# Slot attention and layer norms with centring on TensorE and folded weights; small weights of all stages loaded early

## What is computed

```
c = LN(ctx, lnkv_g, lnkv_b);  k = c @ wk + bk;  v = c @ wv + bv
slots = q_mu + exp(q_logsig) * layernorm(x)
3 times:
  q = LN(slots, lnq_g, lnq_b) @ wq + bq
  attn = softmax over the slots of (q k^T * sqrt(128)) + 1e-8, then divided by its sum over the context
  slots = slots + (attn @ v) @ wu + bu
  slots = slots + gelu(LN(slots, lnm_g, lnm_b) @ w1 + b1) @ w2 + b2 + cond
  slots = LN(slots, lnp_g, lnp_b)
```

## Time and profile before

| | us |
|---|---|
| median of 3 runs | 4661.4 |
| lowest, highest | 4659.08, 4669.54 |
| the profiled execution | 4675.68 |
| its span in the trace | 4673.9 |

### The profile page before, as it was taken

How to read it: one execution, slowest core, us unless ns; L and a number is a source line. 1 busy time by engine, 2 the same in 40 slices (tenths; PEclk the granted TensorE clock), 3 DMA queues, 4 the chain that set the end, 5 groups by cost and what they waited for, 6 DMA issues and landing times. The chain is left out here.

```text
span 4673.9 us, 82115 instructions
## 1 busy us (share of the span) xinstructions
PE 4081.2 (87%) x25253; PEld 2362.5 (51%) x25314; DVE 2853.7 (61%) x13552; ACT 2300.9 (49%) x6553; POOL 911.0 (19%) x4346
## 2 busy tenths in 40 slices
PE   6789999999999999999988999777888888888868
PEld 2247777777777777777733333322333333333222
DVE  4556666666666666666653444537666666666535
ACT  3335555555555555555543333313555555555423
POOL 0123333333333333333332000300000000011002
PEclk8889999999999999999999999857888888888869
DMA  0000000000000000000001000011111111111100
GB/s 9 24 7 2 2 2 2 2 2 2 2 2 2 2 2 2 2 2 2 2 34 47 1 1 1 28 51 52 45 56 44 56 44 56 56 44 51 37 31 5
DMA packets 48838, 94.55 MB, mean 20 GB/s; under 512 B 11296, under 2 KB 31792, under 8 KB 48144
## 3 DMA queue, kind: packets, MB, share of 16 engines
q1 hardware_dynamic: 48400, 89.29, 5.9%
HBM read 72.94 MB, written 15.39 MB: 19 GB/s over the span
## 5 line engine op out<-in xcount | busy, mean ns | idle before, releaser
L761 PE MATMUL ps<-g_h,w_p 128*128 128x128 f32 x4096 | 918.2, 306 | 0.0
L2091 ACT ACTIVATE t_ex<-ps 128x1024 f32<-128x1024 f32 (+1 forms) x480 | 472.1, 1021 | 571.9 <-PE ps L2038 558.4
L761 PEld LDWEIGHTS ps<-g_h,w_p 128*128 128x128 f32 x4096 | 616.7, 190 | 0.0
L757 PE MATMUL ps<-g_h,w_p 128*128 128x77 f32 x2048 | 456.5, 304 | 171.7 <-DVE g_h L829 155.6
L2186 DVE TENSOR_REDUCE t_ncol<-ps 128x1 f32<-128x512 f32 x768 | 486.5, 683 | 153.2 <-PE ps L2011 152.6
L825 DVE SCALAR_TENSOR_TENSOR g_used<-g_encg,g_e 128x77 f32<-128x77 f32 x3072 | 551.0, 230 | 0.2
L795 ACT ACTIVATE g_th<-ps 128x77 f32<-128x77 f32 x1024 | 242.4, 237 | 528.0 <-PE ps L757 528.0
L871 POOL TENSOR_SCALAR g_z<-g_tzr 128x1 f32<-128x1 f32 x1024 | 196.8, 192 | 1410.0 <-ACT g_tzr L804 1410.0
L757 PEld LDWEIGHTS ps<-g_h,w_p 128*128 128x128 f32 x2048 | 304.5, 188 | 307.6 <-DVE g_h L829 303.9
L776 PE MATMUL ps<-g_th,g_vrep 128*128 128x77 f32 x2048 | 456.5, 305 | 0.5 <-ACT g_th L795 0.5
L834 DVE TENSOR_REDUCE g_ntop<-ps 128x1 f32<-128x77 f32 x1024 | 244.3, 239 | 338.1 <-PE ps L776 338.1
(11 more groups left out here) (433 smaller groups left out, 6762.5 us busy)
## 6 DMA issues: line engine op xcount, KB each, us to landing
t_qst<-t_turn_q SPq DMA_DIRECT2D x288, 96.0 KB
t_kst<-t_turn_k SPq DMA_DIRECT2D x144, 96.0 KB
t_turn_q<-t_part SPq DMA_DIRECT2D x24, 384.0 KB, 2.5
t_turn_k<-t_part SPq DMA_DIRECT2D x12, 384.0 KB, 3.3
t_wf<-in_t_wf SPq DMA_DIRECT2D x6, 514.5 KB, 5.6
m_experts<-in_experts SPq DMA_DIRECT2D x1, 3072.0 KB, 12.4
t_wa<-in_t_wa SPq DMA_DIRECT2D x6, 448.0 KB, 3.4
t_wx<-in_t_wx SPq DMA_DIRECT2D x6, 448.0 KB, 4.2
```

The lines of the kernel that those rows point to most:

```text
L757: M(att[c], w["att_h"], h[t % 2][:, c:c + 1].broadcast_to([P, S]), start=False, stop=True, skip_group_check=True).then_inc(*st.sem("att", c))
L761: return M(G[c][:, g], weights, h[t % 2][:, c:c + 1].broadcast_to([P, P]), start=False, stop=last, skip_group_check=True)
L2091: A(ex[0:kw, slot[pf, c, l, n]], ps[0:kw, at:at + 2], ACT.Exp, scale=SCALE).then_inc(*st.sem(f"{pf}e{n}", c))
```

## The change

Layer norms in `slots_stage` and `norm_stage`: TensorE multiplies by `center` = identity minus 1/128, so that the centred values stand in PSUM. ScalarE squares them from there, VectorE multiplies them from there by the reciprocal deviation. The subtraction is gone, and a lane has two banks. Gains and shifts are folded: the `q` norm centres through `center` scaled by `exp(q_logsig)` or `lnp_g`, with a column added inside Square and the product; `lnq_g` and the softmax scale stand in the keys, `lnm_g` in `w1`, `lnm_b` in its bias. The table load of Ln and Exp comes once at the stage's start and after each Gelu.

The query matmul is folded into the keys (`wqT` times `kT`), the output matmul into the values (`vT` times `wu`). What the biases add to the logits is a row for each context token, split into three bf16 parts and added by a small bf16 matmul (`crow`, `ones3`). The reciprocal of the context sum is `exp(-ln)` on ScalarE. The prologue has more steps, and most of them stand between the first centring and the first logits.

Weights: every pack has a place in SBUF from the start. `setup_stage` issues the first two, the block ahead of the second stage the other six, behind its experts. `load_stage` waits for nothing and is there for the three mixtures alone; the wait for a pack stands in `release`. In `rms_stage` the table load moves ahead of the Squares.

```diff
+def center_pe(k, pe, st, name, src, width, banks, ready, weights=None):
+    for c in range(B):
+        ready(c)
+        k.nc.tensor.matmul(k.ps[:, banks[c][0], 0:width], k.center[:] if weights is None else weights, src(c),
+                           start=True, stop=True).then_inc(*st.sem(name + ".cent", c))
+def variance_pe(k, pe, st, name, width, banks, sq=None, rnd=0):
...
+        k.nc.tensor.matmul(k.ps[:, banks[c][1], 0:width], k.mean_w[:], sq[:, c, 0:width], start=True, stop=True)\
+def square_act(k, act, st, name, width, banks, sq=None, rnd=0, shift=0.0):
...
+        k.nc.scalar.activation(sq[:, c, 0:width], k.ps[:, banks[c][0], 0:width], ACT.Square, bias=shift)\
+def rstd_act(k, act, st, name, width, banks, rstd=None, rnd=0):
...
+        k.nc.scalar.activation(rstd[:, c, 0:width], k.ps[:, banks[c][1], 0:width], ACT.Ln, bias=k.eps[:, 0:1])\
...
+        k.nc.scalar.activation(rstd[:, c, 0:width], rstd[:, c, 0:width], ACT.Exp, scale=-0.5)\
+def norm_dve(k, dve, st, name, dst, width, banks, rstd=None, rnd=0, shift=None):
...
+            op = k.nc.vector.tensor_tensor(dst(c), cent, rstd[:, c, 0:width], ALU.mult)
...
+            op = k.nc.vector.scalar_tensor_tensor(out=dst(c), in0=cent, scalar=shift, in1=rstd[:, c, 0:width],
+                                                  op0=ALU.add, op1=ALU.mult)
@@ setup_stage
+            for pack in packs[0:2]:
+                pack.load(sp, k)
             sp.wait_ge(landed, 16 * 3)
...
+            nc.gpsimd.tensor_tensor(k.center[:], k.ident[:], k.mean_w[:], ALU.subtract).then_inc(made, 1)
@@ load_stage
-            sp.dma_start(whole[:], k.dram[pack]).then_inc(landed, 16)
-            if experts is not None:
-                experts.load(sp)
-            sp.wait_ge(landed, 16)
+            experts.load(sp)
+            for pack in packs:
+                pack.load(sp, k)
@@ slots_stage, TensorE
+            M(ps[:, 3, 0:1], k.center[:], w["q_mu"], start=True, stop=True)
+            M(ps[:, 3, 1:2], k.center[:], w["lnp_b"], start=True, stop=True)
+            M(ps[:, 3, 2:3], w["w1"], w["lnm_b"], start=True, stop=True).then_inc(*one.sem("cols"))
+            center_pe(k, pe, pre, "x", lambda c: k.x[:, c], T, XB, lambda c: None)
+            center_pe(k, pe, pre, "c", lambda c: k.ctxT[:, c], S, CB, lambda c: None)
...
             for r in range(ROUNDS):
+                center_pe(k, pe, st, "q", lambda c: n[:, c], T, QB, first if r == 0 else
+                          (lambda c: pe.wait_ge(*st.at("p.norm", c, r - 1))), cg[:, min(r, 1)])
+                if r == 0:
...
+                        M(ps[:, 2 + 4 * c, 0:S], w["wk"], cn[:, c], start=True, stop=True).then_inc(*pre.sem("key", c))
...
+                        M(ps[:, 2 + 4 * c, 0:S], w["wv"], cn[:, c], start=True, stop=True).then_inc(*pre.sem("val", c))
...
+                        M(ps[:, 2 + 4 * c, 0:S], w["wqT"], kT[:, c], start=True, stop=True).then_inc(*pre.sem("wqk", c))
+                variance_pe(k, pe, st, "q", T, QB, rnd=r)
+                if r == 0:
...
+                        M(ps[0:S, 2 + 4 * c, 0:1], kT[:, c], w["bq"], start=True, stop=False)
+                        M(ps[0:S, 2 + 4 * c, 0:1], kraw[:, c], w["lnq_b"], start=False, stop=True).then_inc(*pre.sem("cc", c))
...
+                        M(ps[0:S, 2 + 4 * c, 0:D], vT[:, c], w["wu"], start=True, stop=True).then_inc(*pre.sem("vw", c))
...
+                        M(ps[0:3, 2 + 4 * c, 0:S], c3[0:S, c], identb[0:S, 0:S], start=True, stop=True).then_inc(*pre.sem("ct", c))
...
-                    nc.tensor.matmul(ps[:, 1 + 4 * c], w["wq"], y[:, c], start=True, stop=True).then_inc(*st.sem("query", c))
...
-                    nc.tensor.matmul(ps[0:S, 2 + 4 * c], kT[:, c], q[:, c], start=True, stop=True).then_inc(*st.sem("logit", c))
+                    M(ps[0:S, 2 + 4 * c], crow[0:3, c], ones3[0:3], start=True, stop=False)
...
+                    M(ps[0:S, 2 + 4 * c], kk[:, c], y[:, c], start=False, stop=True).then_inc(*st.sem("logit", c))
...
-                    nc.tensor.matmul(ps[:, 1 + 4 * c], v[0:S, c], e[0:S, c], start=True, stop=True)\
+                    M(ps[:, 1 + 4 * c], vw[0:S, c], e[0:S, c], start=True, stop=True).then_inc(*st.sem("upd", c))
...
-                    nc.tensor.matmul(ps[:, 2 + 4 * c], w["wu"], y[:, c], start=True, stop=True).then_inc(*st.sem("wu", c))
@@ slots_stage, ScalarE, in each round
+                    A(rsum[:, c], ps[:, 3 + 4 * c], ACT.Ln).then_inc(*st.sem("cs.ln", c))
...
+                    A(rsum[:, c], rsum[:, c], ACT.Exp, scale=-1.0).then_inc(*st.sem("cs.inv", c))
...
+                    A(hid[:, c], ps[:, 1 + 4 * c], ACT.Gelu, bias=b1p[:, 0:1]).then_inc(*st.sem("gelu", c))
+                nc.scalar.preload_act_table_set("natural_log_exp_and_others")
@@ slots_stage, VectorE, in each round
-                    nc.vector.tensor_scalar(q[:, c], ps[:, 1 + 4 * c], w["bq"], None, ALU.add).then_inc(*st.sem("qT", c))
...
-                    nc.vector.reciprocal(rsum[:, c], ps[:, 3 + 4 * c]).then_inc(*st.sem("rsum", c))
...
-                    nc.vector.scalar_tensor_tensor(out=mid[:, c], in0=ps[:, 2 + 4 * c], scalar=w["bu"], in1=slots[:, c],
...
+                    V.tensor_tensor(mid[:, c], upd[:, c], slots[:, c], ALU.add).then_inc(*st.sem("mid", c))
...
+                        V.tensor_scalar(slots[:, c], n[:, c], w["lnp_g"], bu2[:, 1:2], ALU.mult, ALU.add).then_inc(*st.sem("slots", c))
@@ norm_stage
-            ln_pe(k, pe, st, "x", lambda c: k.x[:, c], T, (0, 4), 2, lambda c: None)
+            center_pe(k, pe, st, "x", lambda c: k.x[:, c], T, BANKS, lambda c: None)
+            variance_pe(k, pe, st, "x", T, BANKS)
...
-            ln_act(k, act, st, "x", T, (0, 4), 2)
+            nc.scalar.preload_act_table_set("natural_log_exp_and_others")
+            square_act(k, act, st, "x", T, BANKS)
+            rstd_act(k, act, st, "x", T, BANKS)
...
-            ln_dve(k, dve, st, "x", lambda c: k.x[:, c], lambda c: dst[:, c], T, (0, 4), 2)
+            norm_dve(k, dve, st, "x", lambda c: dst[:, c], T, BANKS)
@@ rms_stage
+            nc.scalar.preload_act_table_set("natural_log_exp_and_others")
             for c in range(B):
                 nc.scalar.activation(k.sq[:, c], src[:, c], ACT.Square).then_inc(*st.sem("sq", c))
-            nc.scalar.preload_act_table_set("natural_log_exp_and_others")
@@ build
+        setup_stage(k, packs)
+        k.release(packs[0].landed)
...
-                    load_stage(k, whole, f"p{n}", experts)
+                    load_stage(k, packs[2:] if stage is layer1_stage else [], experts)
...
-                    load_stage(k, whole, f"p{n}")
...
+            k.release(packs[n + 1].landed if n + 1 < len(packs) else None)
```

More of the change, by code:

```diff
@@ L89, in semaphore, with release @@
         return self.signals[-1]
-    def release(self):
+    def release(self, needed=None):
+        if needed is not None:
+            self.nc.sync.wait_ge(needed, 16)
         self.nc.clear_and_free_semaphores(self.signals)
@@ L110 @@
 LN_PE, LN_ACT, LN_DVE = "{0}.mean {0}.var", "{0}.sq {0}.ln {0}.rstd", "{0}.cent {0}.norm"
-LNA_DVE = LN_DVE + " {0}.affine"
+LNC_PE, LNC_DVE = "{0}.cent {0}.var", "{0}.norm"
+def center_pe(k, pe, st, name, src, width, banks, ready, weights=None):
[4 more added lines that the diff above has]
+def variance_pe(k, pe, st, name, width, banks, sq=None, rnd=0):
+    sq = k.sq if sq is None else sq
+    for c in range(B):
+        pe.wait_ge(*st.at(name + ".sq", c, rnd))
+        k.nc.tensor.matmul(k.ps[:, banks[c][1], 0:width], k.mean_w[:], sq[:, c, 0:width], start=True, stop=True)\
+            .then_inc(*st.sem(name + ".var", c))
@@ new lines, in norm_dve @@
+def norm_dve(k, dve, st, name, dst, width, banks, rstd=None, rnd=0, shift=None):
+    rstd = k.rstd if rstd is None else rstd
+    for c in range(B):
+        dve.wait_ge(*st.at(name + ".rstd", c, rnd))
+        cent = k.ps[:, banks[c][0], 0:width]
+        if shift is None:
+            op = k.nc.vector.tensor_tensor(dst(c), cent, rstd[:, c, 0:width], ALU.mult)
+        else:
+            op = k.nc.vector.scalar_tensor_tensor(out=dst(c), in0=cent, scalar=shift, in1=rstd[:, c, 0:width],
+                                                  op0=ALU.add, op1=ALU.mult)
+        op.then_inc(*st.sem(name + ".norm", c))
@@ L180, in _, with __init__, load, load_stage @@
             pool.wait_ge(made, 5)
-def load_stage(k, whole, pack, experts=None):
+            nc.gpsimd.tensor_tensor(k.center[:], k.ident[:], k.mean_w[:], ALU.subtract).then_inc(made, 1)
+            pool.wait_ge(made, 6)
+class Pack:
+    def __init__(self, k, ctx, name):
+        self.name = name
+        self.whole, self.parts = k.weights(ctx, name)
+        self.landed = k.nc.alloc_semaphore("landed_" + name)
+    def load(self, sp, k):
+        sp.dma_start(self.whole[:], k.dram[self.name]).then_inc(self.landed, 16)
+def load_stage(k, packs, experts):
     with ExitStack() as ctx:
-        landed = k.semaphore("landed_" + pack)
```

(28 more changed lines are left out.)

239 lines of the change are left out of this document (149 added, 90 removed).

## The result

The changed kernel ran in 4592.8 us (median of 4 runs, 4590.1 to 4598.3), beside 4660.2 for the kernel before in the same comparison (4 runs, 4658.0 to 4669.5). The ratio is 0.9853 with an interval of 0.9836 to 0.987. The forecast was 4585 with a range of 4566 to 4612. Two later comparisons of the same two programs, each on another occasion, gave 0.9814 (0.9801 to 0.9828) and 0.9809 (0.979 to 0.9829).

The account below looks back on a forecast made before the run. The slot stage was read as a serial chain where each engine waits for the one before. Slot stage -51.7, weights -18.5, norms -6.4, warm starts -2.5, RMS +2.6 make -76.5: 4661.4 becomes 4585 us, range 4566 to 4612.

Parts of the forecast that it names:

- The slot stage: Serial chain of prologue and three rounds: instructions taken out are worth their whole time, -51.7 us.
- the six stretches of the sum: A slot-stage round at full clock, cut in six from centring to next round: gains together 19.8, round 28.2 us.
- the fifth: Slot round, `w1` to the second `w2` sum: 5.4 us becomes 4.4, since Gelu's load now ends last.
- no pause over 1.7 us, so little half clock: Slot rounds: TensorE is busy for two thirds, so the clock seldom falls; 1.0 us a round added.
- The entries: Stage starts: SP's waits for packs and eight issues go, -22.0; moved issues cost +2.9 at second stage; sum -18.5 us.
- Norms and warm starts: Norms at six stage heads, -6.4 us; TensorE perhaps starting at full clock behind four shorter entries, -2.5.
- A: TensorE stays at half clock in the slot stage: 4615 us, half the effect 4600; chance 0.12 for 4596 to 4618.
- granted clock over 0.9 in the rounds: Slot rounds: sign that would show TensorE mostly at full clock, as forecast.
- B: Stage entries keep their time, as a barrier waits for something else; gain of 22 lost: 4604 us, chance 0.06.
- C: All slot rounds at full clock (-4.3) and stages that start at full clock (-5): 4575 us, chance 0.15.
- D: Recurrent stage: operands in new SBUF places read slower; 0.15 us a step eats the gain, 0.2 gives 4687; chance 0.01.
- E: Loads or bias row stay on the path, e.g. prologue 35 us and Gelu's load fully exposed: 4597, chance 0.06.

Follow-up runs that it names:

- after_again: The changed kernel run once more with no edit: 4593.8 us, ratio 0.9814 to the kernel before.
- after_third: The changed kernel run a third time with no edit: 4572.9 us, ratio 0.9809 to the kernel before.
- after: The changed kernel in its first comparison and profile: 4592.8 us, ratio 0.9853 to the kernel before.
- packs_in_slots: The changed kernel with packs 2 to 7 issued by SP at the start of the slot stage, not ahead of the second stage: 4589.5 us, ratio 0.9803.
- before_again: The kernel before run once more, unchanged, as a control with a new profile: 4671.3 us, ratio 1.0.
- the extra product: The changed kernel with one more 512-column product behind each round's logits, its result unread: 4593.1 us, and 4586.9 when repeated.

## Why the prediction was right

The size came out right in the span (77.4 against 76.5). The median moved by 67.5, 9.0 less, since the runs of before beside it lay mostly at their lower level. The parts came out mostly for the reasons given, but with errors that cancel.

**The slot stage**: forecast -51.7, measured -45.9, and -50.5 and -49.8 in the other two profiles. In the first, 5.8 were missing: one part was better than forecast, three were worse.
- The prologue was counted too long. First maximum 23.3 after the start, forecast 26.5: 3.2 better. Up to `q`'s centring the chain took 10.5 (forecast 10.3), and the ten splits 1.7 (2.0; 23.55 to 25.25). Mis-sized are the constant column (2.0 forecast; its matmuls start at 22.79 and the first split at 23.55), `vws`, `slots` and `crow` (2.3 against 1.5, to 26.79), and the 1.7 for half clock, which came only with the logits. The prediction's sum is also off by itself: its terms make 24.6, not 24.8.
- Rest of the first round, 27.5 against 22.8: 4.7 worse. At full clock it would be 22.8 (29.4 less 6.6), so this is the clock, low from 28 to 44. In after_again it is 27.3 and in after_third 26.8, 4.5 and 4.0 too long. Forecast were 1.3.
- Second round 31.4 against 29.2, third 34.1 against 32.0: 2.2 and 2.1 worse. Both at full clock, in after_again, are 29.4 and 31.9.

In after_again the second round can be held against the six stretches of the sum, all at full clock (starts of the rows named in the prediction): 6.6, 3.7, 4.6, 4.2, 5.2 and 5.1, where 6.65, 3.65, 4.5, 4.1, 4.4 and 4.9 were forecast. A reader's start 1.12 to 1.17 behind its product, on which these sums rest and which the earlier trace rows don't show, is 1.16 here (66.55 to 67.71 in after). One is wrong, the fifth: I had Gelu's first activation 1.7 behind `w1`, and it comes 2.5 behind. The forecast had the load start as the last Exp ends, as it does before at 107.78. In after it starts behind the wait for the product, as the row at 79.71 shows: 1.21 after `w1`. That is 0.8 a round. The 1.0 a round put in for the clock is right for the second and third round by luck: each is either undisturbed (0) or some 2 longer, and 5 of 12 in six profiles are the latter. For the first round 1.3 was put in and 2.2 to 4.7 came. So in the slot stage the step that failed is "no pause over 1.7 us, so little half clock". The pauses were as forecast (1.37), and the clock fell in some rounds behind one of them, and in every profile of the changed kernel behind the thin stretch ahead of the first logits.

**The entries**: forecast -18.5, measured -19.4 (-2.1 at the start, +3.3 at the second stage, -20.6 in the six others). The waits went as forecast, and the six issues cost somewhat more than said: 0.63 each in place of 0.48, and by the packs_in_slots run 3.8 to 5.0 in all, where 2.9 were charged. That the moved issues had to be charged where they land was the step that kept the sum honest; without it the forecast would be 3 us lower.

**Norms and warm starts**: forecast -8.9 together, measured -11.3. One that starts at half clock gains 0.9 to 1.9 (174.21 to 183.97 before; 129.48 to 137.34 after), and one that starts at full clock 3.0: the stage at 2445.65 took 6.4 against 9.4, where 8.1 was forecast for a norm at full clock. At half clock throughout it is 8.8 (2301.07 to 2309.89), as forecast. The experiments part the two terms: 7.3 for the norms with the old entries (forecast 6.4), and 4.0 more with the short ones (forecast 2.5). **RMS** was +2.6 in forecast and in measurement.

**The rest** was to stay: the recurrent stage moved by -2.3 (2055.2 to 2058.6 over all profiles, so it didn't move), the last transformer by +2.9, and these and smaller ones together by -3.4, which is scatter. Added up: -45.9 - 19.4 - 11.3 + 2.6 - 3.4 = -77.4.

**The rivals.** A, half clock in the slot stage: true in part, 8.9 us of the first profile's stage (4.7 + 2.0 + 2.2), 4.5 of after_again's and 6.2 of after_third's, where the forecast held 3.3; it was priced at 15 to 30 and is a matter of degree, not a case. The sign "granted clock over 0.9 in the rounds" failed in after (0.89 in the second round, 0.50 for 16 us of the first). B, entries that keep their time, is out: 1.1 us at the recurrent stage where it was 5.4. C, all at full clock: no profile shows it for the whole slot stage, but after_third's median, 4572.9, is near its 4575 for another reason, the ternary stage. D, slower recurrent steps, is out: the block takes 2029.6 in after and 2030.0 in before_again. E is out for the prologue (23.3 where it had 35), but its other half is true: Gelu's load is fully exposed.

The switch of tables: the Trainium skill ("ScalarE: Activation LUTs", What ACT_TABLE_LOAD costs) gives 2.66 us, a load of 1.28 and a drain of 1.38. The trace agrees on the load and shows no drain: in after the load at 79.71 takes 1.28 and the Gelu follows at 81.00, 0.01 later, and the load at 82.28 starts 0.02 after the Gelu ends.

What stays open: what decides the granted clock in an execution. No run changed it in the ternary stage on purpose; that the 11 us between the two levels of before's times come from there is likely, since one stage can be 17 us longer or shorter with no edit, but both profiles of before are at the upper level, so it isn't shown. Nor is it tried whether Gelu's load is hidden again without the second wait, some 0.8 us a round by the sum.

## What to carry to other kernels

Sum a serial chain row by row, and charge every moved issue to the queue that it lands on: this gave 77 us, with every part within 6. Some of that is luck: the slot stage fell short by 5.8, and the norms, the entries and the scatter of stages that nobody touched made up 6.7. By the medians the gain was 67.5 in the first comparison and 85.4 and 95.4 in the others, so one comparison can't confirm such a sum to better than some 15 us. Where an engine is idle anyway (SP in the slot stage), put the loads there and not in a short entry that waits for it; and put a table load behind the last work that doesn't need it if that work waits for nothing (3.3 us in RMS). Look in the trace whether a load that nobody placed lies ahead of its wait or behind it. Before one explains a difference of 10 us between two kernels, one has to know how much the same program moves by itself in stages that nobody touched.

## What the runs showed that was not expected

- One program's TensorE stays at 1.2 GHz in a stretch in which it is fully busy for 30 us, in one execution, and is at 2.4 in another (0.50 against 0.94 and 1.00 in the stretches above), which makes 16 us of a span of 4590.
- A pause of 1.37 us between two products is followed by half clock in some rounds and not in others, with the same instructions: after at 68 us 0.51, after_again 1.00. Of six profiles without the extra product, the second round was 29.4 long in three and 31.4 to 31.6 in three; with it, 29.4 in three of three, so the product itself cost nothing in the chain. For this round three are few for a proof; the whole stage is clearer (above).
- A VectorE reciprocal in the chain costs more than its rows say: 18 us in the rounds where the rows alone give 14, since its duration is TensorE's pause as well.
- A table load that nobody placed started ahead of the wait for its input in the kernel before (107.78) and behind it in the changed one (79.71), which has a second wait there.
- An issue on SP took 0.48 us for an expert load in the earlier trace rows, 0.63 for a pack behind such loads (3.75 for six), and 0.46 for a pack at the start of the slot stage (2.76 for six).
